# Four message hops that gather neighbours on TensorE instead of by indirect DMA

## The chip, the cores and the metric

The kernel runs on one core of one Trainium2 chip. The metric is the device time of one execution in microseconds (us), lower is better. Before the change three runs gave 6633.33, 6638.75 and 6645.05 us; the median is 6638.75.

## What is computed

A graph has 3125 nodes of 128 features and 100,000 edges `src -> dst`, sorted by `dst`. The reference is an attention layer with five hops of message passing, a feed-forward layer, and three graph convolutions. The part that matters here is this (feature rows `f` are split in 8 heads of 16):

```python
e = leaky_relu(fh[src] * ft[dst], 0.2)           # per edge and head, then a softmax over the edges of a target
a = ex / esum[dst]                               # (100000, 8): one share per edge and head
f = fe
for _ in range(5):
    msg = f[src] * a[:, :, None]                 # gather the source's row, weigh it by head
    agg = segment_sum(msg, dst, num_segments=n)  # sum over the edges of each target
    f = 0.85 * agg + 0.15 * fe
...                                              # layer norm, feed-forward, then three times:
norm = dinv[src] * w * dinv[dst]                 # graph convolution, with self loops
out = segment_sum((x @ W)[src] * norm, dst) + b
```

## The kernel before

**Tiling.** Nodes lie in 25 buckets of 125, one node a partition. Edges, in order of target, are cut into items of 128 edges, one edge a partition, so that every item has targets of one bucket only: 816 items, handled in 204 groups of 4 (51 turns of a loop with 4 slots). For a group, VectorE compares the edges' places in their bucket with a row of numbers, which gives a 128x125 one-hot matrix for each item (`onehots`, L1135). One matmul per item with that matrix as weights (L878) adds the item's 128 message rows into the PSUM columns of its target bucket. The bucket's number is a register that TensorE's instruction stream loads for each group (`buckets_of`, L448). All seven banks hold the sums of a hop; bank 7 is free for other things.

**Stages.** (1) Layer norms, projections, tables. (2) The score stage: per group, GpSimd gathers 4x128 rows of a table by indirect DMA (L673), TensorE turns the one-hots and multiplies, VectorE makes the scores, and the gathered `fe` half is written to a DRAM buffer `edge_fe`. (3) Softmax scans. (4) Hop 0 reads `edge_fe` back group by group through SyncE's queue (L560). (5) Hops 1 to 4: after each hop the new `f` goes to a DRAM table `tab_f`, ScalarE copies the row numbers of a group to `stage` (L736), GpSimd issues four indirect DMAs a group (L673), VectorE makes the one-hots (L1135) and weighs the rows (L1192), TensorE sums. (6) Feed-forward and three convolutions.

**Work tucked into the hops.** The convolutions use a dense adjacency, which is built during hops 1 to 4 in 352 steps, 88 a hop, one with every second group. A step is, on VectorE, one comparison for 4 items (L1150) and four scaled one-hots (L1154), then on TensorE four products (L867), then on VectorE four chained additions (`build_sums`, L1165), each waiting for the one before, and four DMAs to the buffer `adj` (L574). Hop 1 also sums the edge weights of each target with a one-column matmul per item (L875).

**What sets the order.** Each engine's instructions stand in the order of the code, joined by semaphores; there is no planner. [...] 

## Time and profile before

| | |
|---|---|
| Median of three runs | 6638.75 us |
| The profiled execution's own time | 6636.84 us |
| Its span in the trace | 6635.0 us |
| TensorE, VectorE, GpSimd busy | 62%, 53%, 60% of the span |
| Chain that ended last | GpSimd 42%, issue 31%, TensorE 12%, VectorE 7%, DMA 6% |
| Mean granted TensorE clock | 0.607 of full speed |

A busy share is an average over stages with different limits, so the rows below are taken from single stages. In a row, a name such as `L673` is the line of the kernel's file; PE is TensorE, PEld its weight load, DVE is VectorE, ACT is ScalarE, POOL is GpSimd, SP is SyncE, and a q behind an engine's name is its sequencer. [...]

### The profile page before, as it was taken

Reading aid. Unit: us, or ns where it says so; the run is one execution under the profiler, and the core shown is the slowest. Engines: PE = TensorE matmul, PEld = TensorE weight load, DVE = VectorE, ACT = ScalarE, POOL = GpSimd, SP = SyncE. Lnnn points to the kernel's source line nnn. Section 1 sums busy time; section 2 is a strip of 40 time slices with the busy share of each in tenths; the row PEclk is TensorE's granted clock in tenths of the full one; section 3 lists DMA queues with packets and bytes.
Section 4 is the critical chain, followed back from the end, with each engine's and each line's share of the span. In section 5 each row is a group of like instructions: output and inputs, shape, how many; then the busy total and the mean of one; then the engine's idle time right before and its main releaser. Section 6 shows DMA issues by size and latency. Waiting matters only on the chain.

```text
span 6635.0 us, 87679 instructions
## 1 busy us (share of the span) xinstructions
PE 4108.7 (62%) x19868; PEld 3666.2 (55%) x19869; DVE 3545.8 (53%) x7014; ACT 423.6 (6%) x1409; POOL 3995.5 (60%) x4073
## 2 busy tenths in 40 slices
PE   3655645624778888865555544555544555555899
PEld 1444534524668888855545534545443545443899
DVE  7765656677855555435555534555544555544211
ACT  0111111110000000000000000000000000001000
POOL 0577767711047777767777767777776777773000
PEclk9655555557965555555656556565655565656999
DMA  2344464513632222222222212222222222222576
GB/s 58 109 139 146 144 147 135 148 39 117 182 102 77 78 78 77 76 59 77 77 78 77 78 58 76 78 78 77 79 65 68 79 77 78 78 72 76 208 272 231
DMA packets 538438, 671.65 MB, mean 101 GB/s; under 512 B 102388, under 2 KB 423419, under 8 KB 528412
## 3 DMA queue, kind: packets, MB, share of 16 engines
q1 hardware_dynamic: 391970, 345.94, 17.1%
q0 software_dynamic: 143008, 320.73, 16.8%
q10 hardware_dynamic: 3418, 4.48, 0.2%
q8 instruction: 18, 0.29, 0.0%
q14 instruction: 24, 0.20, 0.0%
HBM read 511.17 MB, written 160.80 MB: 101 GB/s over the span
## 4 chain that ended last, share of the span: by engine, by line
POOL 42%; issue 31%; PE 12%; DVE 7%; DMA 6%; SPq 1%; ACT 1%; DVEq 1%; POOLq 0%; ACTq 0%; PEldq 0%; PEld 0%
POOL U L673 42%; PE ps L1091 6%; PE ps L878 3%; DMA U<-edge_fe 2%; DMA U<-tab_f,stage 2%; DVE U L1192 1%; DVE U L1491 1%; DVE U L1463 1%; DVE U L1111 1%; DMA U<-tab_he,stage 1%; PE ps L954 1%; DMA edge_fe<-U 0%; SPq L580 0%; PE ps L867 0%; DMA tab_f<-U 0%
## 5 line engine op out<-in xcount | busy, mean ns | idle before, releaser
L673 POOL DMA_INDIRECT U<-tab_f,stage x3224 | 3102.6, 962 | 1352.6 <-issue 964.1
L878 PE MATMUL ps<-U 128*125 128x128 f32 x8160 | 2051.7, 407 | 1140.3 <-DVE U L1192 1137.4
L878 PEld LDWEIGHTS ps<-U 128*125 128x125 f32 x8160 | 1681.4, 293 | 1282.1 <-issue 1275.9
L1135 DVE TENSOR_TENSOR U<-dloc,iota_p 128x500 f32<-128x500 f32 x1225 | 840.2, 686 | 1974.1 <-DMA U<-tab_f,stage 1919.6
L673 POOL DMA_INDIRECT U<-tab_he,stage x806 | 850.9, 1056 | 438.5 <-issue 246.5
L867 PE MATMUL ps<-gap 128*128 128x125 f32 x2816 | 706.9, 430 | 388.3 <-DVE gap L1165 388.3
L867 PEld LDWEIGHTS ps<-gap 128*128 128x128 f32 x2816 | 630.0, 329 | 460.1 <-issue 460.1
L1192 DVE TENSOR_TENSOR U<-U,ex_it 128x512 f32<-128x512 f32 x1020 | 705.3, 692 | 0.0
L1165 DVE SCALAR_TENSOR_TENSOR gap<-gap,U,ps 128x125 f32<-128x125 f32 x1408 | 483.5, 343 | 154.7 <-DVE gap L1165 79.6
L979 PE MATMUL ps<-U 125*128 x1632 | 422.4, 440 | 210.5 <-ACT U L773 210.5
L875 PEld LDWEIGHTS ps<-w_it,U 128*125 128x125 f32 x1632 | 435.8, 327 | 187.4 <-issue 186.6
L979 PEld LDWEIGHTS ps<-U 125*128 125x128 f32 x1632 | 363.3, 328 | 270.1 <-issue 270.1
L736 ACT COPY stage<-src_it 128x4 int32 (+1 forms) x1023 | 197.6, 193 | 4922.6 <-PE ps L878 4319.9
L875 PE MATMUL ps<-w_it,U 128*125 x1632 | 365.5, 293 | 152.4 <-DVE U L1192 151.9
L972 PE MATMUL ps<-ident,U 128*125 128x128 f32 x816 | 244.1, 454 | 259.1 <-DVE U L1135 258.5
L1154 DVE TENSOR_SCALAR gap<-iota_p,U,raw 128x125 f32<-128x125 f32 x1408 | 389.6, 343 | 0.0
L972 PEld LDWEIGHTS ps<-ident,U 128*125 128x125 f32 x816 | 188.2, 321 | 308.3 <-DVE U L1135 307.3
L1380 DVE TENSOR_TENSOR U<-U,ps 128x512 f32<-128x512 f32 x204 | 140.7, 690 | 378.0 <-DMA U<-tab_he,stage 323.0
L1150 DVE TENSOR_TENSOR gap<-U,iota_p 128x512 f32<-128x512 f32 x352 | 244.2, 694 | 0.2
L1588 DVE TENSOR_TENSOR U<-ps,gap 128x125 f32<-128x125 f32 x75 | 21.7, 289 | 380.9 <-PE ps L1091 380.9
L1091 PE MATMUL ps<-ex_it,U 125*128 125x125 f32 x1500 | 171.5, 274 | 2.3 <-DVE ex_it L1582 2.2
L1091 PE MATMUL ps<-U 125*128 125x125 f32 x1500 | 172.4, 273 | 0.0
(236 smaller groups left out, 2097.1 us busy)
## 6 DMA issues: line engine op xcount, KB each, us to landing
adj<-gap SPq DMA_DIRECT2D x1408, 64.0 KB
edge_fe<-U SPq DMA_DIRECT2D x204, 256.0 KB, 2.5
U<-edge_fe SPq DMA_DIRECT2D x204, 256.0 KB, 2.9
U<-tab_f,stage POOLq DMA_INDIRECT x3224, 2.5
ex_it<-adj SPq DMA_DIRECT2D x30, 1600.0 KB, 6.1
U<-adj SPq DMA_DIRECT2D x30, 1600.0 KB, 6.1
fe_a<-adj SPq DMA_DIRECT2D x15, 1600.0 KB, 6.1
U<-tab_he,stage POOLq DMA_INDIRECT x806, 2.9
```

Source lines behind the costliest of these rows:

```text
L673: pool.indirect_dma_start(to[:, k, j, :], None, table, bass.IndirectOffsetOnAxis(ap=stage[:, k, j:j + 1], axis=0)).then_inc(got[k], 16)
L867: mm = nc.tensor.matmul(ps[:, 7 * BANK + j * CELL:7 * BANK + (j + 1) * CELL], hot_p[:, u, j, :], prod[:, u, j, :], start=True, stop=True)
L875: nc.tensor.matmul(ps[0:BN, bass.ds(b + W_SUMS, 1)], hot[:, k, j, :], w_it[:, bass.ds(r * PER_ITER + (k * G + j), 1)], start=False, stop=F ...
L878: mm = nc.tensor.matmul(ps[0:BN, bass.ds(b * F, F)], hot[:, k, j, :], ga[:, k, j, :], start=False, stop=False, skip_group_check=True)
L972: t = nc.tensor.transpose(bank(k % 2)[0:BN, j * P:(j + 1) * P], hot[:, k, j, :], ident[:])
L979: mm = nc.tensor.matmul(bank(2 + k % 2)[:, j * F:(j + 1) * F], hot_t[:, k % 2, j, :], nb_pad[0:BN, bass.ds(b, 1), :].rearrange("p b f -> p ...
L1091: mm = nc.tensor.matmul(bank(u, BN).rearrange("p (w d) -> p w d", d=WN), rows_[0:BN, b, :], cells[:, :, b, :], start=(b == 0), stop=(b == ...
L1135: return v.tensor_tensor(to[:, (k + ahead) % SLOTS], dloc[:, bass.ds(item_of(r, k, ahead), G)].unsqueeze(2).to_broadcast([P, G, BN]), iota ...
L1150: v.tensor_tensor(hot_p[:, u], win_p[:, bass.ds(i, BG)].unsqueeze(2).to_broadcast([P, BG, P]), iota_p[:].unsqueeze(1).to_broadcast([P, BG, ...
L1154: ins = v.tensor_scalar(prod[:, u, j, :], iota_bn, win_b[:, bass.ds(i, 1)], win_w[:, bass.ds(i, 1)], ALU.is_equal, ALU.mult)
L1165: ins = v.scalar_tensor_tensor(out=win_acc[:, u, j, 0:CELL], in0=before, scalar=win_same[:, bass.ds(win_item(s, r, u, j), 1)], in1=ps[:, 7 ...
L1192: v.tensor_tensor(rows_, rows_, by, ALU.mult).then_inc(msgs_ready, 1)
```

## The change

The edges get a second order, by pair of source bucket and target bucket: 1408 items in place of 816, each with sources of one bucket and targets of one. With it a hop's gather is a product: a one-hot matrix of sources (bf16, 125x128) times the bucket's rows of `f`. `f` is split into three bf16 parts, so an item takes three products, which add up in PSUM bank 7.

- **Score stage**: in its first 25 turns VectorE and TensorE also count each edge's place in the new order (`source_buckets`, `rank_step`, `rank_known`, `places`), and VectorE finds the pairs of the new items (`pair_items`).
- **Hop 0** still reads `edge_fe`. From its 32nd group on, each group is paired with one building step (172 of the 352); the edge weights are summed here. Beside it ScalarE packs the edges' shares, sources and targets into records, and GpSimd scatters these to their new places with 806 indirect DMAs.
- **After hop 0** the 180 steps that are left run by themselves. Then GpSimd gathers the records in the new order (11 DMAs) and TensorE turns them.
- **Hops 1 to 4** no longer use GpSimd. Each is 352 steps of 4 items (`cell_pass`): TensorE gathers the next step's items (12 products) and adds up this step's messages (4 float32 matmuls); VectorE compares sources for every second step, makes the next step's target one-hots, and then weighs the rows that lie in bank 7. Between hops ScalarE and VectorE split `f` (`split_parts`, `split_rest`).

The core of the diff; parts that repeat, buffers and semaphores are left out:

```diff
-            def sum_pass(s):
-                for r0, r1 in ((0, BUILD_ITERS), (BUILD_ITERS, ITERS)) if s else ((0, ITERS),):
-                    sum_groups(s, r0, r1, s > 0 and r0 == 0)
-            def sum_groups(s, r0, r1, building):
+            def build_cells(t, r, k):
+                pe.wait_ge(prod_ready, r * SLOTS + (t + k + 1))
+                pe.wait_ge(acc_ready, r * SLOTS + (t + k + 1))
+                for j in range(BG):
+                    mm = nc.tensor.matmul(cells_at(j), hot_p[:, k % BSLOTS, j, :], prod[:, k % BSLOTS, j, :],
+                                          start=True, stop=True)
+                mm.then_inc(cell_sums, 1)
+            def sum_groups(r0, r1):
                 with pe.Fori(r0, r1) as r:
                     for k in range(SLOTS):
-                        if building and k % 2 == 0:
-                            u = k // 2
-                            pe.wait_ge(prod_ready, r * BSLOTS + (steps_before(s) + u + 1))
-                            pe.wait_ge(acc_ready, r * BSLOTS + (steps_before(s) + u + 1))
-                            for j in range(BG):
-                                mm = nc.tensor.matmul(ps[:, 7 * BANK + j * CELL:7 * BANK + (j + 1) * CELL],
-                                                      hot_p[:, u, j, :], prod[:, u, j, :], start=True, stop=True)
-                            mm.then_inc(cell_sums, 1)
+                        if r0 >= BUILD_FROM:
+                            build_cells(-BUILD_FROM * SLOTS, r, k)
                         buckets = buckets_of(pe, item_of(r, k))
-                        pe.wait_ge(msgs_ready, r * (2 * SLOTS) + (msgs_before(s) + 2 * (k + 1)))
+                        pe.wait_ge(msgs_ready, r * (2 * SLOTS) + (msgs_before(0) + 2 * (k + 1)))
                         for j, b in enumerate(buckets):
-                            if s == 1:
-                                nc.tensor.matmul(ps[0:BN, bass.ds(b + W_SUMS, 1)], hot[:, k, j, :],
-                                                 w_it[:, bass.ds(r * PER_ITER + (k * G + j), 1)],
-                                                 start=False, stop=False, skip_group_check=True)
+                            nc.tensor.matmul(ps[0:BN, bass.ds(b + W_SUMS, 1)], hot[:, k, j, :],
+                                             w_it[:, bass.ds(r * PER_ITER + (k * G + j), 1)],
+                                             start=False, stop=False, skip_group_check=True)
                             mm = nc.tensor.matmul(ps[0:BN, bass.ds(b * F, F)], hot[:, k, j, :], ga[:, k, j, :],
                                                   start=False, stop=False, skip_group_check=True)
                         mm.then_inc(groups_done, 1)
...
+            def cell_pass(s):
+                pe.wait_ge(split_done, BANKS * s)
+                pe.wait_ge(src_hots, (s - 1) * PLOADS + 1 + PRING)
+                gather_items(0, cell_regs(pe, 0))
+                for r0, r1 in cut(0, PITERS - 1, PITERS):
+                    with pe.Fori(r0, r1) as r:
+                        for k in range(PSTEPS):
+                            last = r0 and k == PSTEPS - 1
+                            i = r * (PSTEPS * G) + k * G
+                            of = None if last else cell_regs(pe, i + G)
+                            to = cell_regs(pe, i + PITEMS)
+                            pe.wait_ge(weighted, group_of(s, r, k) + 1)
+                            if not last:
+                                if k % 2:
+                                    pe.wait_ge(src_hots, load_of(s, r, (k + 1) // 2) + (1 + PRING))
+                                gather_items((k + 1) % PSTEPS, of)
+                            pe.wait_ge(dst_hots, group_of(s, r, k) + 1)
+                            for j, b in enumerate(to):
+                                mm = nc.tensor.matmul(ps[0:BN, bass.ds(b * F, F)], dst_hot[:, k % PRING, j, :],
+                                                      msg[:, k % PRING, j, :], start=False, stop=False,
+                                                      skip_group_check=True)
+                            mm.then_inc(scattered, 1)
+            def gather_items(k, cells):
+                for j, b in enumerate(cells):
+                    for n in range(PARTS_F):
+                        mm = nc.tensor.matmul(bank(7)[:, j * F:(j + 1) * F], src_t[0:BN, k // 2, k % 2 * G + j, :],
+                                              split[0:BN, n, bass.ds(b, 1), :].rearrange("p b f -> p (b f)"),
+                                              start=(n == 0), stop=(n == PARTS_F - 1))
+                mm.then_inc(gathered, 1)
...
+            def rank_step(r):
+                pe.wait_ge(rank_hot, r + (1 - RANK_FROM))
+                for n, m in enumerate((before_m, ones_b)):
+                    for half in range(2):
+                        mm = nc.tensor.matmul(bank(4 + 2 * n + half, HALF), m[:], src_hot[:, half * HALF:(half + 1) * HALF],
+                                              start=True, stop=True)
+                mm.then_inc(rank_sums, 1)
...
-            def message_pass(s):
-                for r0, r1 in cut(0, 1, FULL_ITERS, BUILD_ITERS, ITERS) if s else cut(0, ITERS):
-                    if s and r0 == BUILD_ITERS:
-                        build_sums(s, BUILD_ITERS - 1, BSLOTS - 1)
-                    message_groups(s, r0, r1, s > 0 and r0 < BUILD_ITERS)
-                dve.wait_ge(groups_done, SLOTS + (s + 1) * GROUPS)
...
-            def message_groups(s, r0, r1, building):
+                dve.wait_ge(acc_ready, r * SLOTS + (t + k + 2))
+            def message_groups(r0, r1):
+                t = -BUILD_FROM * SLOTS
                 with dve.Fori(r0, r1) as r:
                     for k in range(SLOTS):
-                        if building and k % 2 == 0:
-                            build_factors(s, r, k // 2)
-                            if k or r0:
-                                build_sums(s, r if k else r - 1, (k // 2 - 1) % BSLOTS)
-                        if s == 0:
-                            dve.wait_ge(loaded[k], r * 16 + 16)
-                        else:
-                            dve.wait_ge(got[k], got_at(s, r, k, r0))
+                        if r0 >= BUILD_FROM:
+                            build_factors(t, r, k)
+                            if k or r0 > BUILD_FROM:
+                                build_sums(t, r, k - 1)
+                        dve.wait_ge(loaded[k], r * 16 + 16)
                         onehots(hot, r, k).then_inc(msgs_ready, 1)
                         i = item_of(r, k)
                         rows_ = ga[:, k].rearrange("p g (h d) -> p (g h) d", h=HEADS)
                         by = ex_it[:, bass.ds(i, G), :].rearrange("p g h -> p (g h)").unsqueeze(2).to_broadcast(
                             [P, G * HEADS, HD])
                         v.tensor_tensor(rows_, rows_, by, ALU.mult).then_inc(msgs_ready, 1)
+            def compare_sources(s, r, q, ahead=0):
+                dve.wait_ge(loaded[(q + ahead) % PRING], r * 16 + 16 * (ITERS + (s - 1) * PITERS + 1 + (q + ahead) // PRING))
+                dve.wait_ge(gathered, 2 * load_of(s, r, q + ahead) + 2)
+                v.tensor_scalar(src_t[0:BN, (q + ahead) % PRING].rearrange("p i e -> p (i e)"),
+                                ids[0:BN, (q + ahead) % PRING, :], pidx[0:BN, 0:1], None,
+                                ALU.is_equal).then_inc(src_hots, 1)
+            def dst_onehots(s, r, k, ahead=0):
+                dve.wait_ge(scattered, group_of(s, r, k + ahead) + 1)
+                v.tensor_tensor(dst_hot[:, (k + ahead) % PRING],
+                                dst_c[:, bass.ds(r * (PSTEPS * G) + (k + ahead) * G, G)].unsqueeze(2).to_broadcast([P, G, BN]),
+                                iota_bn.unsqueeze(1).to_broadcast([P, G, BN]), ALU.is_equal).then_inc(dst_hots, 1)
+            def weigh(s, r, k):
+                dve.wait_ge(gathered, group_of(s, r, k) + (1 + 2 * PRING))
+                dve.wait_ge(scattered, group_of(s, r, k) + 1)
+                by = ex_it[:, bass.ds(r * (PSTEPS * G) + k * G, G), :].rearrange("p g h -> p (g h)").unsqueeze(
+                    2).to_broadcast([P, G * HEADS, HD])
+                v.tensor_tensor(msg[:, k % PRING].rearrange("p g (h d) -> p (g h) d", h=HEADS),
+                                bank(7).rearrange("p (x d) -> p x d", d=HD), by, ALU.mult).then_inc(weighted, 1)
+            def cell_pass(s):
+                compare_sources(s, 0, 0)
+                dst_onehots(s, 0, 0)
+                for r0, r1 in cut(0, PITERS - 1, PITERS):
+                    with dve.Fori(r0, r1) as r:
+                        for k in range(PSTEPS):
+                            if k % 2 == 0 and not (r0 and k == PSTEPS - 2):
+                                compare_sources(s, r, k // 2, 1)
+                            if not (r0 and k == PSTEPS - 1):
+                                dst_onehots(s, r, k, 1)
+                            weigh(s, r, k)
+                dve.wait_ge(scattered, PRING + s * PGROUPS)
+            def split_rest(n):
+                def part_of(k):
+                    b0, b1 = bank_buckets(k)
+                    return b0, b1, rest[0:BN, k, 0:(b1 - b0) * F].rearrange("p (b f) -> p b f", f=F)
+                for k in range(BANKS):
+                    b0, b1, to = part_of(k)
+                    dve.wait_ge(split_high, n * BANKS + k + 1)
+                    v.tensor_tensor(to, na[0:BN, b0:b1], split[0:BN, 0, b0:b1], ALU.subtract).then_inc(split_link, 1)
+                for k in range(BANKS):
+                    b0, b1, to = part_of(k)
+                    dve.wait_ge(split_mid, n * BANKS + k + 1)
+                    v.tensor_tensor(split[0:BN, 2, b0:b1], to, split[0:BN, 1, b0:b1], ALU.subtract).then_inc(split_done, 1)
+                dve.wait_ge(split_done, (n + 1) * BANKS)
...```

[...]

```order
L448 ISA
L448 TENSOR_LOAD bucket_row
L872 REGISTER_ALU
L878 ISA
L878 MATMUL ps<-U 125x128
```

TensorE, one step of hops 1 to 4 now, from the last of the four adding matmuls (L1103) of one step to the first of the twelve gathering products (L1112) of the next:

```order
L1103 ISA
L1103 MATMUL ps<-U 125x128
L553 ISA
L553 TENSOR_LOAD U
L553 ISA
L553 TENSOR_LOAD U
L1096 REGISTER_ALU
L1099 ISA
L1112 ISA
L1112 MATMUL ps<-U 128x128
```

A step now has two register loads, for the source and the target buckets, and 16 matmuls, each behind a register instruction of its own; a group before had one load and four.

VectorE, hop 0, the end of a building step and a message group, then the next step's beginning (L1425 are the chained additions, L1402 the one-hots, L1449 the weighting, L1409 and L1413 the factors of the next step). In the kernel before, hop 0 has the lines L1135 and L1192 alone, which are L1402 and L1449 here.

```order
L1425 ISA
L1425 SCALAR_TENSOR_TENSOR gap<-gap,U,ps 128x125
L1432 REGISTER_ALU
L1402 ISA
L1402 TENSOR_TENSOR U<-dloc,iota_p 128x500
L1449 ISA
L1449 TENSOR_TENSOR U<-U,ex_it 128x512
L1409 ISA
L1409 TENSOR_TENSOR gap<-U,iota_p 128x512
L1413 ISA
L1413 TENSOR_SCALAR gap<-iota_p,U,raw 128x125
```

The building step has moved from every second group of hops 1 to 4 to every group of hop 0 from the 32nd on.

## Rows read from the trace of the kernel before

**Rows 1.** The profile page, groups of instructions: busy, mean ns | idle before, releaser

```profile
L673 POOL DMA_INDIRECT U<-tab_f,stage x3224 | 3102.6, 962 | 1352.6 <-issue 964.1
```

**Rows 2.** Waits, all engines: us in total, times, longest

```profile
DVE U L1135 <- DMA U<-tab_f,stage: 1919.6, 811, 19.8
```

**Rows 3.** Chain that ended last, in order of time: ends of hops 0 and 4

```profile
1878.83 3.88 DVE U L1534 x7
...
6060.52 3.89 DVE U L1534 x7
```

**Rows 4.** Windows: hop 0, part of hop 1, hop 2, convolutions

```profile
core 0: us, PE busy (x) PEld busy (x) DVE busy (x) ACT busy (x) POOL busy (x), PEclk, DMA share, GB/s
1550.00:1885.00 335.00, 241.36 (x1635) 203.50 (x1635) 280.96 (x420) 0.77 (x4) 22.46 (x11) 0.93 0.58 171
2205.00:2525.00 320.00, 281.27 (x1271) 272.04 (x1271) 174.52 (x414) 12.18 (x63) 242.91 (x254) 0.50 0.28 78
2930.00:3980.00 1050.00, 565.62 (x2357) 503.33 (x2355) 524.29 (x1212) 39.95 (x207) 776.66 (x806) 0.56 0.26 74
6168.00:6635.00 467.00, 449.50 (x3948) 443.88 (x3947) 64.24 (x232) 30.09 (x76) 0.00 (x0) 0.99 0.67 249
```

**Rows 5.** Sequencer instructions by line, 1605.2 to 1606.4 us (hop 0, one group)

```profile
L878 PEldq FUSED_REGOPS  x4: 46/46/46, 1605.3 to 1605.7; - x4
...
L448 PEldq FUSED_REGOPS  x1: 46/46/46, 1605.8 to 1605.8; - x1
L448 PEldq TENSOR_LOAD <-bucket_row x1: 334/334/334, 1605.9 to 1605.9; - x1
...
L872 PEldq ALU_OP  x1: 32/32/32, 1606.3 to 1606.3; - x1
```

**Rows 6.** The same for L979, 600 to 604 us (score stage, one group)

```profile
L979 PEldq FUSED_REGOPS  x4: 55/55/55, 602.7 to 603.1; - x4
```

**Rows 7.** Timeline of hop 0: start us, us, engine line op

```profile
1601.13 0.67 DVE L1135 TENSOR_TENSOR U<-dloc,iota_p 128x500 f32<-128x500 f32 x1
...
1601.72 0.68 DVE L1192 TENSOR_TENSOR U<-U,ex_it 128x512 f32<-128x512 f32 x1
1602.33 0.67 DVE L1135 TENSOR_TENSOR U<-dloc,iota_p 128x500 f32<-128x500 f32 x1
```

**Rows 8.** Timeline of hop 2, a group with a building step

```profile
3200.59 0.68 DVE L1150 TENSOR_TENSOR gap<-U,iota_p 128x512 f32<-128x512 f32 x1
...
3202.22 0.34 DVE L1165 SCALAR_TENSOR_TENSOR gap<-gap,U,ps 128x125 f32<-128x125 f32 x1
3202.71 1.33 DVE L1165 SCALAR_TENSOR_TENSOR gap<-gap,U,ps 128x125 f32<-128x125 f32 x3 [0.15 <-DVE gap L1165]
...
3204.18 2.04 PE L867 MATMUL ps<-gap 128*128 128x125 f32 x8 [1.29 <-DVE gap L1165]
```

**Rows 9.** Timeline of hop 1, TensorE: two items with the weight column

```profile
2302.60 0.77 PE L878 MATMUL ps<-U 128*125 128x128 f32 x2
...
2303.45 0.77 PE L878 MATMUL ps<-U 128*125 128x128 f32 x2
```

**Rows 10.** Timeline, TensorE: clearing seven banks after hop 0

```profile
1882.76 3.16 PE L851 MATMUL ps<-zeros 1*128 1x512 bf16 x7 [8.94 <-DVE U L1534]
```

**Rows 11.** Timeline of the score stage: VectorE's last and first work of a group

```profile
599.43 0.69 DVE L1389 TENSOR_REDUCE ex_it<-U 128x512 f32 x1
...
604.95 0.69 DVE L1389 TENSOR_REDUCE ex_it<-U 128x512 f32 x1
```

**Rows 12.** Groups of instructions with shapes kept apart: the nearest to the new ones

```profile
L1463 DVE TENSOR_TENSOR_SCAN U<-gap,U 128x6528 f32<-128x6528 bf16 x3 | 41.3, 13758 | 9.5 <-ACT U L793 9.4
...
L1277 DVE TENSOR_SCALAR_CACHE_REDUCE U<-U 128x782 f32<-128x782 f32 x25 | 24.2, 968 | 0.9
...
L1417 DVE TENSOR_SCALAR_CACHE_REDUCE U<-U,win_it 128x625 f32<-128x625 f32 x11 | 9.5, 864 | 0.4
...
L1029 PE MATMUL ps<-ident,U 128*128 128x128 f32 x51 | 8.1, 336 | 23.3 <-ACT U L806 23.3
```

More of the change, by code:

```diff
@@ L44 @@
 AHEAD = SLOTS - 1
-TABLES = HOPS - 1
 WN = 5
@@ new lines, in _ @@
+            with sp.Fori(0, BUILD_FROM + 1) as r:
+                for k in range(SLOTS):
+                    load_group(r, k)
+            sp.wait_ge(targets_ready, 1)
+            first = -(BUILD_FROM + 1) * SLOTS
+            with sp.Fori(BUILD_FROM + 1, ITERS) as r:
+                for k in range(SLOTS):
+                    load_group(r, k)
+                    store_step(first, r, k)
+            sp.wait_ge(cell_out, 16 * 2)
+            sp.dma_start(cell_row, cell_d.rearrange("(a n) -> a n", a=1)).then_inc(cell_in, 16)
@@ new lines, in _ @@
+            act.wait_ge(built, 1)
+            for k in range(PK):
+                act.wait_ge(rec_turned, k + 1)
+                at_ = slice(k * P, (k + 1) * P)
+                banks = [3 * (k % 2) + n for n in range(3)]
+                nc.scalar.copy(ex_it[:, at_, HALF_HEADS:], bank(banks[1]).rearrange("p (h i) -> p i h", i=P)
+                               ).then_inc(rec_kept_a, 1)
+                nc.scalar.copy(dst_c[:, at_], bank(banks[2], P)).then_inc(rec_kept_a, 1)
+            for s in range(HOPS - 1):
+                split_parts(s)
```

509 lines of the change are left out of this document (416 added, 93 removed).

## The prediction

> **What bounds the kernel now.** I read the chain of waits first, then the page's groups, then windows by stage, then the timeline of one group in each stage. From the end of hop 0 to the end of hop 4 the trace takes 6060.5 - 1878.8 = 4182 us [rows 3], two thirds of the span. There GpSimd sets the pace: an indirect DMA costs it (3102.6 + 964.1) / 3224 = 1.26 us with its issue gap [rows 1], so 806 of them are 1017 us, nearly a whole hop. VectorE mostly waits for those rows, 1920 us in all [rows 2], and in hop 2 it is busy 524 of 1050 us, with the building steps in it [rows 4]. So the building is free today, and hop 0, which does without GpSimd, takes about 335 us [rows 4]. The change takes GpSimd out of hops 1 to 4. What counts is what a step of the new hops costs on TensorE and VectorE, and what the building costs once nothing covers it.
>
> **The new step of hops 1 to 4.** There are 352 steps a hop.
>
> VectorE has one 500-element comparison and one 512-element weighting. These start 0.6 us apart when nothing holds them [rows 7]. The source comparison, 1024 bf16 elements in every second step, is not in the trace: at the pace of the 6528-element scan it would be the dearest, 2.1 ns an element or 2.2 us, at the 782-element comparison's it is 1.24 ns or 1.3 us [rows 12], so at most 0.65 to 1.1 us a step. VectorE needs 1.5 to 2.3 us a step.
>
> TensorE's array has 12 bf16 products of 128 columns and 4 float32 matmuls, which are 8 halves. [...]
>
> TensorE's sequencer has the most. In one group of hop 0 its rows can be followed: four register instructions that stand ahead of a matmul each, from 1605.3 to 1605.7, then at 1605.8 the register instruction of the load, the load itself at 1605.9 (334 ns) and the next instruction at 1606.3 [rows 5]. So a matmul with a register costs 0.125 us of sequencer time, and a load 0.5 us, whatever the array does. In the score stage, where the register picks the operand that streams through, as in the new gather, four such rows stand from 602.7 to 603.1 and last 55 ns instead of 46 [rows 6], which makes 0.133 us. The new step has two loads, 12 gathering products with a register each, and 4 adding matmuls with one each; the wait values and the loop's end add some 0.15 us (I take 0.1 us for each register instruction that stands alone). The sum is 2 x 0.5 + 12 x 0.133 + 4 x 0.125 + 0.15 = 3.25 us. A group of the kernel before needs 4 x 0.125 + 0.5 + 0.1 = 1.1 us, which lies below VectorE's 1.2 us, so nothing waits for it today.
>
> The round trip must fit too, since there is one bank for gathered rows: weighting 0.69 us, the release of TensorE (3204.04 to 3204.18, 0.14 [rows 8]), the 12 products as the sequencer issues them, 1.6 us, and some 0.4 us until the last is done and VectorE starts: 2.8 us, below 3.25. I take 3.25 us a step, the sequencer's sum. From below 3.0 us (0.115 us a product and no standing instructions), from above 3.6 us (waits that I don't see).
>
> [...]
>
> A hop is 352 x 3.25 = 1144 us, and between hops come the sums, the two halves of the split, and the first gather. That is 21 instructions of VectorE at 0.6 us, since ScalarE's copies run beside them, and about 5 us until the first weighting: 18 us. Four hops: 4 x 1162 = 4648 us against 4182, **+466 us**. The gather by products is no faster than the gather by DMA.
>
> **The building loses its cover.** On VectorE a step runs from 3200.59 to 3204.04 [rows 8], and 0.2 us more until the next instruction can start: 3.7 us. With the message group's 1.2 us that is 4.9 us a group of hop 0. TensorE in the same group has four items with the weight column, 0.85 us each at 1.2 GHz [rows 9], and the four products, 8 halves or 1.7 us, together 5.1. In hop 1, the only stretch with these three kinds of work, the granted clock is 0.50 throughout [rows 4], so I take 5.2 us for 172 groups, and 3.4 us for the 32 without a step: 894 + 109 + 5 = 1008 us against 335 [rows 4], less 2 us of lead: **+675 us**. At 2.4 GHz VectorE would set 4.9 us, and the 32 groups take 56 us, together 113 us less.
>
> The 180 steps after hop 0 pass the work to and fro: the additions need the products, the products the additions before. Additions 1.82 us (3202.22 to 3204.04), 0.14 until TensorE starts, products 2.04 us [rows 8], 0.1 back: 4.1 us, while the factors of the next step are made beside the products. 180 x 4.1 = **+738 us**; at 2.4 GHz 3.7 us and 72 us less. Nothing else runs then that the end depends on: the 806 scatters need 806 x 1.26 = 1016 us from hop 0's start on GpSimd and end before this building does, so I cost them at nothing. They would show only if a scatter took over twice as long.
>
> **Smaller terms.** Counting in the score stage: per turn, for 25 turns, two scans of 408 elements at 2.1 ns [rows 12] and six passes over 408 to 816 elements at about 1.1 to 1.2 ns, some 7 us. A turn is four groups of 5.5 us, of which VectorE spends five instructions of about 0.7 us each [rows 11], 3.5 us a group: room for 8 us, so these are hidden in the main. Not hidden are 13 passes over 816 elements ahead of the first group, 12 us, and the search for the pairs, 11 comparisons at 0.9 us [rows 12] and some 25 small instructions, 25 us, of which GpSimd's lead of three groups hides a part; with places in between I take **+60 us**, from 20 to 130. Records: 11 rounds, each nine turns on TensorE at 0.3 us [rows 12], copies and a DMA: **+50 us**, from 25 to 80. The tail loads `x` later, and two small instructions stand alone: **+7 us**.
>
> **Sum.** 466 + 675 + 738 + 60 + 50 + 7 = 1996 us. The profiled execution took 6636.84 us, 0.03% off the median shown, so 8633 us: **8630 us**, slower by 30%. With all low ends (3.0 us a step, 2.4 GHz in the building, the small terms low) 8030 us; with the high ends 9220 us. As they will not all fall together, the likeliest case's own range is 8200 to 9050 us.
>
> **Rivals.**
>
> *The array sets the step, not the sequencer.* If register instructions were worked off ahead while matmuls wait, the step would be the round trip with products at array pace: 0.69 + 0.14 + 12 x 0.054 + 0.4 = 1.9 us to, at a float32 half's 0.12 us each, 2.7. Half-way, 2.3 us, gives 8633 - 0.95 x 1408 = 7300 us. For it speaks that the sequencer runs ahead of the array in hop 0; against it that its rows stand 0.125 us apart even then [rows 5]. Chance 0.07. [...]
>
> *The step is a chain.* If the sequencer can't prepare the next loads while VectorE weighs, because the wait for the target one-hots or the four matmuls holds it, the round trip and the rest add up: 2.8 + 0.5 + 1.0 = 4.3 us, 8633 + 1.05 x 1408 = 10,110 us. Against it: the order has the loads ahead of the wait for the weighting. Chance 0.05.
>
> *Faster.* The register work is hidden as in the first rival, and TensorE keeps 2.4 GHz from hop 0 to hop 4, so that the step is 1.85 us and the building loses 185 us: 8633 - 1.4 x 1408 - 185 - 40 = 6440 us. The point from which the change pays is a step of 1.83 us with the other terms as they stand, 2.0 us with these low. For it speaks that hop 0 ran at 0.93 [rows 4]; against it the spacing of the sequencer's rows again. Chance 0.04.
>
> **How the numbers follow.** The sequencer's case has 0.84; the rivals 0.07, 0.05 and 0.04. The range 8100 to 9100 leaves out all three rivals, 0.16, and the far ends of the likeliest case, about 0.04. A change within 0.2% is what a measurement of this kernel can't tell from none. Faster by over 0.2%: 0.04. Within 0.2%: 0.01, a step of 1.83 us by chance. Slower: 0.95.
>
> **What would show it.** In the changed profile: a pass of 352 steps takes 1050 to 1200 us with VectorE and the array busy about half of it; the matmuls of the gather start some 0.13 us apart, and between two steps TensorE's array sits idle behind its own sequencer and not behind VectorE; hop 0 takes about 1000 us, the building after it some 740 us with TensorE and VectorE in turns, and GpSimd's scatters end before it. The forecast is wrong if a step takes under 2.8 us, if waits for VectorE's weighting lead the list of TensorE's waits, or if the scatters are what hop 0 or the records wait for.

## The result, and the profile after

The changed kernel takes 8699.5 us (median of 4 runs, 8694.9 to 8705.2), the kernel before 6636.9 us on the same chip: a ratio of 1.311, 95% interval 1.308 to 1.313. The forecast was 8630 us.

The span is cut by events that both traces have: the first weighting of hop 0, the bank sums that end a hop, the first split, the end. The two first weightings are these rows, of the kernel before and of the changed one (the columns: line, engine, operation, tiles, count: ns shortest/median/longest, first and last start in us).

```profile
L1192 DVE TENSOR_TENSOR U<-U,ex_it x1020: 679/686/3631, 1548.1 to 6057.6; 128x512 f32<-128x512 f32 x170
```

```profile
L1449 DVE TENSOR_TENSOR U<-U,ex_it x204: 680/686/3648, 1623.8 to 2608.2; 128x512 f32<-128x512 f32 x102
```

Hop 0 starts 76 us later. The changed kernel's chain of waits (start, us, what) gives the ends of hop 0 and of hop 4, beside [rows 3], and what follows hop 4:

```profile
2614.15 3.88 DVE U L1977 x7
```

```profile
8091.54 3.89 DVE U L1977 x7
8095.51 34.15 DMA U<-in_x
```

Its stages by windows: hop 0, the building after it, a part of hop 3, the load of `x`, the convolutions. Beside [rows 4] the reader sees a hop 0 three times as long at a clock of 0.50 in place of 0.93, and hops at the full clock (1.00) in which VectorE is busy 45% of the time. TensorE's 578 of 700 us there is no measure of what its array needs: each gathering product stands in the trace for 228 ns, and with fixed buckets (below) the same products start 0.056 us apart.

```profile
core 0: us, PE busy (x) PEld busy (x) DVE busy (x) ACT busy (x) POOL busy (x), PEclk, DMA share, GB/s
1623.00:2614.00 991.00, 986.32 (x4647) 984.01 (x4645) 794.62 (x1956) 91.06 (x724) 769.90 (x721) 0.50 0.40 105
2618.00:3385.00 767.00, 368.91 (x1448) 322.15 (x1448) 559.33 (x1628) 12.95 (x90) 95.80 (x96) 0.50 0.22 64
5000.00:5700.00 700.00, 577.75 (x4266) 449.80 (x4266) 314.82 (x534) 0.00 (x0) 0.00 (x0) 1.00 0.10 39
8097.00:8130.00 33.00, 0.00 (x0) 0.00 (x0) 2.06 (x1) 0.00 (x0) 0.00 (x0) 0.50 0.67 242
8230.00:8696.00 466.00, 449.48 (x3948) 443.85 (x3947) 63.99 (x232) 30.07 (x76) 0.00 (x0) 0.99 0.67 250
```

The list of waits now, beside [rows 2] (us in total, times, longest):

```profile
DVE U L1472 <- PE ps L1112: 2539.1, 1408, 2.6
...
PEld ps L1112 <- issue: 1086.3, 1412, 7.1
...
PE ps L1112 <- DVE U L1455: 418.3, 696, 6.2
...
PE ps L1112 <- issue: 397.9, 701, 1.2
```

VectorE waits 1.8 us a step for the gathering products. What TensorE waits for is put down to its own issue in one half of the steps and to VectorE's source comparison in the other. The timeline of one step lets that be judged; each float32 matmul stands in it as two halves, each with a weight load (L1103, 8 and 8 for four), each bf16 one as one with one (L1112, 12 and 12):

```profile
5000.51 0.69 DVE L1472 TENSOR_TENSOR U<-ps,ex_it 128x512 f32<-128x512 f32 x1 [2.22 <-PE ps L1112]
5001.12 0.48 DVE L1455 TENSOR_SCALAR U<-gap,pidx 125x1024 bf16<-125x1024 bf16 x1
...
5001.98 1.53 PEld L1112 LDWEIGHTS ps<-U 125*128 125x128 bf16 x12 [0.77 <-issue]
5001.99 1.67 PE L1112 MATMUL ps<-U 125*128 x12 [0.59 <-DVE U L1455]
5003.54 0.95 PEld L1103 LDWEIGHTS ps<-U 128*125 128x125 f32 x8
5003.55 1.14 PE L1103 MATMUL ps<-U 128*125 128x128 f32 x8
5003.80 0.69 DVE L1472 TENSOR_TENSOR U<-ps,ex_it 128x512 f32<-128x512 f32 x1 [1.61 <-PE ps L1112]
```

and the rows of TensorE's sequencer in the same stretch, first the loads, then the instruction that sets the value of the wait for the comparison, then the gathering products, as [rows 5] showed them for hop 0:

```profile
L553 PEldq FUSED_REGOPS  x2: 46/46/46, 5000.7 to 5001.2; - x2
L553 PEldq TENSOR_LOAD <-U x2: 332/332/333, 5000.8 to 5001.3; - x2
```

```profile
L1099 PEldq FUSED_REGOPS  x1: 42/42/42, 5001.8 to 5001.8; - x1
```

```profile
L1112 PEldq FUSED_REGOPS  x12: 46/46/60, 5001.9 to 5003.3; - x12
```

The weighting was done at 5001.20 and the comparison at 5001.60, both before the sequencer came to the waits for them (L1099, 5001.8); the gather began at 5001.98, when the second load (5001.3, 332 ns) and the standing instructions behind it were through. Then the twelve register instructions follow, 0.13 us apart (0.131 us from product to product in the mean of all 1408 gathers), and the next four and two loads behind them. In the whole step of 3.28 us the sequencer has no stretch in which it waits. "<-DVE U L1455" names only the last semaphore that came. The sequencer's rows stand in the order in which the code has the lines: L553, L1096 (5001.7), L1099, L1112, L1103 (5003.4 to 5003.9). What the listing of the change has there as `REGISTER_ALU` is an ALU_OP of 32 to 36 ns in them (L1096), and `ISA` a FUSED_REGOPS.

### The profile page after: what moved, and what is told of

It reads as the page before. It is cut to its first block, busy times and chain, and to the rows that moved or that the text cites. A ratio compares the mean times of both kernels' runs of the same rounds, so it can differ in the third digit from the quotient of the medians.

```text
span 8696.7 us, 162184 instructions
## 1 busy us (share of the span) xinstructions
PE 6497.5 (75%) x41703; PEld 5403.9 (62%) x41704; DVE 4863.9 (56%) x9329; ACT 406.2 (5%) x1487; POOL 1742.2 (20%) x1671
## 4 chain that ended last, share of the span: by engine, by line
PE 60%; DVE 15%; issue 15%; POOL 3%; DVEq 3%; DMA 2%; ACT 1%; SPq 1%; POOLq 0%; ACTq 0%; PEldq 0%; PEld 0%
PE ps L1112 27%; PE ps L1103 9%; PE ps L1049 7%; PE ps L1065 6%; PE ps L1358 5%; DVE U L1455 4%; POOL U L821 3%; DVE gap L1425 3%; PE ps L1062 2%; PE ps L1227 2%; PE ps L1220 1%; DVE U L1472 1%; DVE U L1933 1%; DVE U L1905 1%; DMA U<-tab_he,stage 1%
## 5 line engine op out<-in xcount | busy, mean ns | idle before, releaser
L1112 PE MATMUL ps<-U 125*128 x16896 | 2355.1, 228 | 821.4 <-DVE U L1455 418.3
L1112 PEld LDWEIGHTS ps<-U 125*128 125x128 bf16 x16896 | 1628.3, 96 | 1627.0 <-issue 1086.3
L1472 DVE TENSOR_TENSOR U<-ps,ex_it 128x512 f32<-128x512 f32 x1408 | 975.9, 693 | 2539.1 <-PE ps L1112 2539.1
L1103 PE MATMUL ps<-U 128*125 128x128 f32 x11264 | 1607.2, 284 | 0.0
L1103 PEld LDWEIGHTS ps<-U 128*125 128x125 f32 x11264 | 1345.7, 187 | 44.9 <-issue 0.2
L1462 DVE TENSOR_TENSOR U<-raw,iota_p 128x500 f32<-128x500 f32 x1408 | 946.2, 672 | 0.0
L869 POOL DMA_INDIRECT rec_d<-ex_it,stage x806 | 844.8, 1048 | 245.6 <-issue 230.6
L1425 DVE SCALAR_TENSOR_TENSOR gap<-gap,U,ps 128x125 f32<-128x125 f32 x1408 | 487.2, 346 | 272.8 <-PE ps L1049 100.5
L1065 PE MATMUL ps<-U 128*125 128x128 f32 x1632 | 628.1, 489 | 0.0
L1227 PE MATMUL ps<-U 125*128 x1632 | 407.8, 429 | 213.6 <-ACT U L930 213.6
L1065 PEld LDWEIGHTS ps<-U 128*125 128x125 f32 x1632 | 443.1, 332 | 0.0
L1413 DVE TENSOR_SCALAR gap<-iota_p,U,raw 128x125 f32<-128x125 f32 x1408 | 388.5, 346 | 0.0
L1062 PE MATMUL ps<-w_it,U 128*125 x1632 | 344.3, 280 | 4.6 <-DVE U L1449 4.6
L1455 DVE TENSOR_SCALAR U<-gap,pidx 125x1024 bf16<-125x1024 bf16 x704 | 337.2, 479 | 0.1
L1402 DVE TENSOR_TENSOR U<-dloc,iota_p 128x500 f32<-128x500 f32 x409 | 282.5, 691 | 87.1 <-DMA U<-edge_fe 54.4
```

Source lines behind the costliest of these rows:

```text
L869: pool.indirect_dma_start(rec_d, bass.IndirectOffsetOnAxis(ap=stage[:, k, j:j + 1], axis=0), recs[:, k, j, :], None).then_inc(got[k], 16)
L1062: nc.tensor.matmul(ps[0:BN, bass.ds(b + W_SUMS, 1)], hot[:, k, j, :], w_it[:, bass.ds(r * PER_ITER + (k * G + j), 1)], start=False, stop=F ...
L1065: mm = nc.tensor.matmul(ps[0:BN, bass.ds(b * F, F)], hot[:, k, j, :], ga[:, k, j, :], start=False, stop=False, skip_group_check=True)
L1103: mm = nc.tensor.matmul(ps[0:BN, bass.ds(b * F, F)], dst_hot[:, k % PRING, j, :], msg[:, k % PRING, j, :], start=False, stop=False, skip_g ...
L1112: mm = nc.tensor.matmul(bank(7)[:, j * F:(j + 1) * F], src_t[0:BN, k // 2, k % 2 * G + j, :], split[0:BN, n, bass.ds(b, 1), :].rearrange(" ...
L1227: mm = nc.tensor.matmul(bank(2 + k % 2)[:, j * F:(j + 1) * F], hot_t[:, k % 2, j, :], nb_pad[0:BN, bass.ds(b, 1), :].rearrange("p b f -> p ...
```

## The experiments

All later runs were on chips where the kernel before took 6682 to 6710 us, and most were single runs. So the length of a step is read within each trace: from the first to the last of a hop's 352 weightings, divided by 351. In the changed kernel it is 3.278 us, and 3.28 in the three runs below that leave these hops as they are (no building, two banks, `x` early).

The theory (A) is the forecast's: TensorE's sequencer sets the step. The rivals: the array sets it (B), or the wait for VectorE's comparison does (C).

**Fixed buckets, both.**

```
-  gather_items(0, cell_regs(pe, 0))
+  gather_items(0, range(G))
   ...
-  of = None if last else cell_regs(pe, i + G)
-  to = cell_regs(pe, i + PITEMS)
+  of = range(G)
+  to = range(G)
```

> Hops 1 to 4 take fixed buckets (0 to 3) in all their products; no bucket number is read into a register. It leaves out that the right buckets are gathered from and added to; counts and sizes of products, waits, VectorE's work and DMAs stay. Theory A (TensorE's sequencer sets the step of 3.26 us: two register loads and 16 register instructions): these go, and what is left is the round trip through the one gather bank, 0.69 (weighting) + 0.14 (release) + 12 products at 0.06 to 0.08 + 0.4 = 2.0 to 2.3 us a step, total 7000 to 7350 us. Rival B (TensorE's array sets it, or the clock): no change, 8700 us. Rival C (the odd steps wait for VectorE's source comparison, as the list of waits says of L1455): no change, 8650 to 8700 us.

6617.9 us; the step is 1.791 us. The twelve gathering products of one step, with the same array work:

```profile
L1112 PEld LDWEIGHTS ps<-U x12: 97/98/100, 4502.2 to 4502.7; 125*128 125x128 bf16 x12
```

They stand 0.056 us apart instead of 0.131, at the same granted clock of 1.00, and the line has no row of the sequencer left (FUSED_REGOPS x12 in the changed kernel). The step and the total lie under the ranges I gave (2.0 to 2.3 us a step). What is left is the round trip: 0.69 us of weighting, 0.05 (even steps) or 0.13 (odd steps) until the first product, 0.85 for the twelve, 0.15 until VectorE starts. VectorE is now busy 2115 of 2566 us in the hops. B and C fall: the array's work, the comparison and its wait were all left in.

**Fixed buckets, gather alone.** `of` and the first gather take `range(G)`, `to` stays.

> Only the gathering products of hops 1 to 4 take fixed buckets; the adding products keep their registers and one load a step. It leaves out that the right source buckets are gathered. Theory A: one load of 0.5 us and 12 register instructions of 0.129 us go; the sequencer needs 0.5 + 4 x 0.125 + 12 x 0.06 to 0.08 + 0.2 = 1.9 to 2.2 us, the round trip is as with both fixed, so a step of 2.1 to 2.3 us, 7050 to 7350 us, nearly as with both fixed. Rivals B and C: no change, 8650 to 8700 us.

6614.3 us, a step of 1.790 us, as with both fixed and as far under the range. One load and four register instructions a step cost nothing once the gather's are gone: the sequencer is then under the round trip.

**Fixed buckets, adding products alone.** Only `to` takes `range(G)`.

> Only the adding products of hops 1 to 4 take fixed buckets; the gathering keeps its 12 register instructions and one load a step. It leaves out that the sums go to the right target buckets. Theory A by the sequencer's sum alone: 0.5 of the load and some 0.3 of the four register instructions go, step 2.45 us, 7570 us. Theory A with the round trip as the next limit (weighting 0.69 + release 0.14 + two standing instructions 0.2 + 12 products at 0.129 + 0.4 = 2.9 us): the gain stops at 0.35 us a step, 8150 to 8250 us. Rivals B and C: 8650 to 8700 us.

7920.1 us, a step of 2.723 us. The gain is 0.55 us a step: more than the 0.35 that I gave for the round trip, less than the 0.8 of the sequencer's sum. The round trip is there, but 2.7 us, not 2.9: in the median 2.68 us in even steps and 2.76 in odd ones, which have one wait more. Here is an even one; the gather begins 0.15 us after the weighting's end.

```profile
4501.28 0.69 DVE L1472 TENSOR_TENSOR U<-ps,ex_it 128x512 f32<-128x512 f32 x1 [1.06 <-PE ps L1112]
...
4502.12 1.51 PEld L1112 LDWEIGHTS ps<-U 125*128 125x128 bf16 x12 [0.25 <-issue]
...
4503.92 0.69 DVE L1472 TENSOR_TENSOR U<-ps,ex_it 128x512 f32<-128x512 f32 x1 [1.36 <-PE ps L1112]
```

**One part.**

```
-  for n in range(PARTS_F):
+  for n in range(1):
   ...
-      start=(n == 0), stop=(n == PARTS_F - 1))
+      start=(n == 0), stop=True)
```

> The gather makes one bf16 product an item in place of three; it leaves out the two lower parts of the numbers gathered. Theory A: 8 register instructions of 0.129 us less a step, 3.26 - 1.03 = 2.2 us, 7200 to 7300 us, and now the sequencer alone is the limit (the round trip is 1.85 us). Rival B (array): 8 x 0.054 = 0.43 us a step, 8090 us. Rival C: at most the time to the comparison, no change in the odd steps, 8300 us or more.

7267.0 us, a step of 2.26 us. Eight products fewer take 1.02 us off, 0.128 us each: the price of the register instruction, more than twice the array's 0.056.

**Loads of eight.**

```
-  of = None if last else cell_regs(pe, i + G)
-  to = cell_regs(pe, i + PITEMS)
+  if k % 2 == 0:
+      of2 = cell_regs(pe, i + G, 2 * G)
+  of = of2[k % 2 * G:][:G]
+  if k % 2 or k == 0:
+      to2 = cell_regs(pe, i + PITEMS, G if k in (0, PSTEPS - 1) else 2 * G)
+  to = to2[G:] if k and k % 2 == 0 else to2[:G]
```

> The bucket numbers of two steps come by one load of eight registers: one load a step in place of two, alternately for the gathering and the adding products. The computation is whole. Theory A (TensorE's sequencer): a load costs 0.5 us whatever it fetches, so its sum falls from 3.28 to 2.78 us a step; the round trip through the gather bank, 2.72 us as the run with only the adding products fixed showed it, lies just below. Total 8699 - 0.5 x 1408 = 8000 us (7950 to 8080). If a load's cost grows with the registers (0.125 us each) nothing is gained, 8700 us. Rival (the wait for VectorE's source comparison): 8650 to 8700 us.

8425.4 us, a step of 3.075 us: 0.20 us gained instead of 0.50. The row of one load shows why:

```profile
L553 PEldq TENSOR_LOAD <-U x1: 588/588/588, 5001.7 to 5001.7; - x1
```

588 ns for eight registers against 332 for four: 0.064 us a register on top of some 0.08, and 0.19 us between its neighbours and it as before. I had the cost of a load as one number; half of it grows with its length. By these rows 0.24 us a step should be gained; the last 0.04 stay open.

**No building.** The factors, products and additions are taken out of hop 0 and of the loop after it.

> Leaves out the factors, products and additions of all 352 building steps; the stores of the steps are still sent, with old contents. By the terms of the forecast alone: 180 steps after hop 0 go (767 us) and hop 0 falls from 991 to some 340 us, total 8699 - 767 - 650 = 7280 us. But GpSimd's 806 scatters, about 1090 us from hop 0's start, then stand bare, since the records need them: if they do, the first split starts some 1150 us after hop 0's start in place of 1800, total 8050 us (7950 to 8150).

8170.1 us; both sums fail. Hop 0 takes 735 us (1637.6 to 2372.8), not 340, and the first split stands at 2894.0, 1256 us after hop 0's start. Two of its windows, inside hop 0 and behind it (columns as above):

```profile
2000.00:2100.00 100.00, 97.17 (x442) 94.03 (x442) 36.05 (x56) 9.06 (x72) 77.75 (x74) 0.50 0.59 149
...
2373.00:2850.00 477.00, 1.95 (x8) 1.58 (x8) 4.21 (x9) 37.44 (x282) 276.44 (x286) 0.50 0.37 104
```

In hop 0 TensorE is 97% busy at a granted clock of 0.50 with the messages and the weight column alone, 3.6 us a group, though no building is there. And after it the stores set the end, not the scatters, which end at 2733.7:

```profile
DVE dinv L1986 <- DMA adj<-gap: 476.4, 1, 476.4
```

The 180 steps' stores take 2.65 us a step by themselves, no less after the scatters' end (2.69) than beside them (2.64). So of the 660 us by which hop 0 grew, the building makes 255 (990 - 735); 405 are left in hop 0 without it, where TensorE is the limit: the weight column, which the change moves there, and the lower clock together. No run separates the two. From hop 0's start to the first split it is 1256 us here against 1801 in the changed kernel, so faster building could gain at most 545 us as long as its stores are sent as they are.

**Two banks in the building.** Products of even steps go to bank 6, so that they need not wait for the additions of the step before (the additions read the same bank):

```
-  pe.wait_ge(acc_ready, r * SLOTS + (t + k + 1))
+  pe.wait_ge(acc_ready, r * SLOTS + (t + k + 1 - two))
   ...
-      mm = nc.tensor.matmul(cells_at(j), ...
+      mm = nc.tensor.matmul(cells_at(j, 6 if two and k % 2 == 0 else 7), ...
```

> In the 180 building steps after hop 0 the products of even steps go to bank 6 (free then) and those of odd steps to bank 7, so that TensorE's products of a step stand beside VectorE's additions of the step before. The computation is whole. If work passed to and fro is what makes 4.26 us a step, VectorE alone sets it: 3.7 us, 180 x 0.56 = 100 us less, 8600 us (8570 to 8640), the stretch from hop 0 to the records 665 us in place of 767. If VectorE's own chain was the limit already, or the stores are, no change, 8700 us.

8612.6 us; from the hop's sums to the last addition 674 us (2624.0 to 3298.3), 3.75 us a step. That is the time of VectorE's own chain, as forecast, and the difference to 4.28 is what the passing to and fro cost.

**`x` early.**

```
+  act.dma_start(x_sb[1:BN], nodes_of(a["x"])[1:BN]).then_inc(x_again, 16)
   act.wait_ge(hops_done, 1)
-  act.dma_start(x_sb[0:BN], nodes_of(a["x"])).then_inc(x_again, 16)
+  act.dma_start(x_sb[0:1], nodes_of(a["x"])[0:1]).then_inc(x_again, 16)
   ...
-  dve.wait_ge(x_again, 16)
+  dve.wait_ge(x_again, 32)
```

> Rows 1 to 124 of x are loaded while hop 4 runs (the bucket numbers lie only in row 0); row 0 after the hops. The computation is whole. The tail's load of 34 us, which stands bare behind the last sum, falls to some 3 us: 30 us less, 8668 us; from the last sum to the end 575 us in place of 605. If the load's time lay in its own fixed cost, 5 us or less.

8677.2 us; from the last sum to the end 580.7 us, 24.4 less. The one row still costs 7.5 us:

```profile
8098.63 7.49 DMA U<-in_x
```

**The registers on ScalarE.** The fixed gather pointed to a form that keeps the computation: ScalarE, idle in the hops, reads the source bucket's register and copies the bucket's three parts into a ring of four steps, and TensorE gathers from fixed places in it. The next four runs have this, the two banks and the early `x`.

```
   ...
+  of = cell_regs(eng, i + js[0], len(js))
+  eng.wait_ge(gathered, group_of(s, r, k) + (1 + 2 * PRING - PRING))
+  for j, b in zip(js, of):
+      copy(held[0:BN, k % PRING, j], split[0:BN, 0:HELD, bass.ds(b, 1), :]...).then_inc(done, 1)
   ...
-  split[0:BN, n, bass.ds(b, 1), :].rearrange("p b f -> p (b f)"),
+  held[0:BN, k % PRING, j, n, :],
```

With GpSimd copying the fourth item:

> The source bucket's registers move off TensorE: ScalarE (three items of a step) and GpSimd (one) copy the three bf16 parts of an item's source bucket into a ring of four steps, and TensorE gathers from fixed places in it; it reads registers for the adding products alone. With it the two banks in the building and the early load of x. The computation is whole. Theory A (TensorE's sequencer was the limit of the hops, and VectorE with the round trip is the next, 1.79 us a step as the runs with fixed buckets showed): ScalarE's three copies of 384 elements at 0.48 us are 1.45 us and fit, so the step is 1.8 us and the total 8699 - 1.48 x 1408 - 88 - 24 = 6500 us (6450 to 6600), 2% under the kernel before. Rival: the copies become the pace (GpSimd's copy over 1.8 us, or VectorE slowed by it): a step of 2.0 to 2.4 us, 6780 to 7350 us.

6748.9 us against 6693.6, ratio 1.008 (1.006 to 1.010): no gain, and above the 6450 to 6600 us that I gave. The step is 1.97 us instead of 1.8. With ScalarE copying all four:

> The three-part form with ScalarE copying all four items of a step. The computation is whole. ScalarE's copies of 384 elements, 0.48 us each, are 1.93 us a step and become the pace: a step of 1.95 to 2.1 us, 8699 - 1.23 x 1408 - 112 = 6850 us (6730 to 6900). If ScalarE's register load of 0.5 us isn't hidden beside its copies, 2.45 us a step, 7420 us.

6614.9 us (one run), a step of 1.88 us: better than with the help, and under the 1.95 us at which ScalarE's copies were to set the pace. Two rows of ScalarE's and GpSimd's copies in the run with both:

```profile
L1033 ACT COPY U<-U 125x384 bf16 x4224 | 1882.3, 509 | 893.5 <-PE ps L1153 877.3
...
L897 POOL COPY U<-U 125x384 bf16 x1408 | 719.4, 511 | 2115.4 <-PE ps L1153 2038.9
```

Neither engine is the pace there: both wait for TensorE. What differs is one more wait in TensorE's queue, between the weighting's end and the gather. An even step with both buckets fixed, where nothing stands between the two, and an odd step of the run with both copying engines, where three waits do (source one-hots and two semaphores of the copies):

```profile
4501.41 0.69 DVE L1472 TENSOR_TENSOR U<-ps,ex_it 128x512 f32<-128x512 f32 x1
...
4502.16 0.67 PEld L1112 LDWEIGHTS ps<-U 125*128 125x128 bf16 x12 [0.15 <-DVE U L1472]
```

```profile
4502.49 0.69 DVE L1514 TENSOR_TENSOR U<-ps,ex_it 128x512 f32<-128x512 f32 x1 [0.63 <-PE ps L1153]
...
4503.50 0.67 PEld L1153 LDWEIGHTS ps<-U 125*128 125x128 bf16 x12 [0.41 <-POOL U L897]
```

From the weighting's end to the first product it is 0.05 us with none between, 0.32 with three; with one it is 0.13 (fixed buckets, odd steps) and with two 0.22 (ScalarE alone, odd steps). Each costs 0.07 to 0.10 us, and "<-POOL" again names only the last semaphore. Take this stretch off the median step, and 1.69 us is left in even and odd steps of all four runs (both buckets fixed, the gather's fixed, both engines copying, ScalarE alone). So the round trip sets the step in all of them, and not the copies; nor does GpSimd's help slow VectorE, whose weighting takes 693 ns with it and without. The last run tests it.

With one part and ScalarE:

> The same with ScalarE alone and one bf16 part an item in place of three; it leaves out the two lower parts of the numbers gathered, and the splitting of them. ScalarE needs 4 x 0.29 = 1.2 us a step, TensorE's sequencer 0.52 + 4 x 0.125 + 4 x 0.06 + 0.3 = 1.6 us, VectorE 0.6 + 0.6 + 0.2 = 1.4 to 1.6 us. Theory A: a step of 1.65 us, total 8699 - 1.63 x 1408 - 88 - 24 - 40 = 6250 us (6200 to 6450). Rival: VectorE and the round trip do not get below the 1.79 us of the fixed buckets: 6450 us or more.

6049.9 us against 6693.6, ratio 0.904 (0.903 to 0.906), a step of 1.49 us. That is under the range I gave. VectorE is busy 1930 of 2025 us of the hops, and its three kinds of work stand nearly without a gap:

```profile
4201.29 0.48 DVE L1477 TENSOR_SCALAR U<-gap,pidx 125x1024 bf16<-125x1024 bf16 x1
4201.68 0.67 DVE L1484 TENSOR_TENSOR U<-raw,iota_p 128x500 f32<-128x500 f32 x1
4202.27 0.68 DVE L1494 TENSOR_TENSOR U<-ps,ex_it 128x512 f32<-128x512 f32 x1
4202.87 0.67 DVE L1484 TENSOR_TENSOR U<-raw,iota_p 128x500 f32<-128x500 f32 x1
4203.63 0.69 DVE L1494 TENSOR_TENSOR U<-ps,ex_it 128x512 f32<-128x512 f32 x1
```

In the steps with a source comparison VectorE now sets the pace (1.59 us); in the others it still waits some 0.1 us for the gather (4203.54 to 4203.63). I had its step at 1.4 to 1.6 us and still took 1.65.

With the wait for the weighting put last:

```
-  pe.wait_ge(weighted, group_of(s, r, k) + 1)
   if not last:
       ...
       held_wait(group_of(s, r, k) + 1)
+  pe.wait_ge(weighted, group_of(s, r, k) + 1)
```

> The three-part form with ScalarE copying all items, and TensorE's waits for the copies and for the source one-hots put ahead of the wait for the weighting, so that only the last stands in the round trip. The computation is whole. The weighting's end to the first gathering product was 0.23 us there (4501.35 to 4501.58) and 0.13 to 0.16 us with both buckets fixed. Theory A: each standing wait costs the sequencer 0.1 us, and in the round trip this is paid in full; the step falls from 1.88 to 1.79 us, 127 us, total 6490 us (6460 to 6550), ratio to before 0.970. Rival: ScalarE, 93% busy with its copies in the hops, is the pace already: a step of 1.85 us or more, 6570 to 6620 us.

6544.5 us against 6685.4 (5 and 9 runs), ratio 0.978 (0.977 to 0.980): the whole computation, and faster than both kernels. The step is 1.83 us: 0.05 us gained, half of what the theory gave. The other half is not the rival's. The groups of ScalarE's copies without and with the edit:

```profile
L1018 ACT COPY U<-U 125x384 bf16 x5632 | 2459.5, 508 | 188.4 <-PE ps L1138 142.3
```

```profile
L1018 ACT COPY U<-U 125x384 bf16 x5632 | 2459.9, 508 | 117.2 <-PE ps L1139 29.0
```

ScalarE is busy 95% of its time now, and yet it isn't the limit. All of its 117 us of idle time lie ahead of the first of a step's four copies, a little in nearly every step. That copy starts together with VectorE's weighting, when TensorE's gather is done and has left a place in the ring; the four then take 1.75 us:

```profile
4502.06 0.51 ACT L1018 COPY U<-U 125x384 bf16 x1
4502.07 0.69 DVE L1500 TENSOR_TENSOR U<-ps,ex_it 128x512 f32<-128x512 f32 x1 [0.54 <-PE ps L1139]
```

```profile
4502.06 1.75 ACT L1018 COPY U<-U 125x384 bf16 x4
```

They start 0.41 us apart, not the 0.48 that I had taken. In the first nine or more steps of each hop, until the ring is full, ScalarE goes at its own pace, 1.65 us a step and without a gap; from then on it waits, and keeps TensorE's 1.81. What is left stands in TensorE's queue. The wait for the weighting (L1120) is still an instruction of its own ahead of the first product:

```profile
4500.26 0.69 DVE L1500 TENSOR_TENSOR U<-ps,ex_it 128x512 f32<-128x512 f32 x1
...
4501.07 0.69 PEld L1139 LDWEIGHTS ps<-U 125*128 125x128 bf16 x12 [0.21 <-issue]
```

```profile
L1120 PEldq EVENT_SEMAPHORE  x1: 51/51/51, 4501.0 to 4501.0; - x1
```

From the weighting's end to the first product it is 0.115 us in even and odd steps alike, where it was 0.13 and 0.22; the rest of the step is 1.70 us, much as in the other runs. The round trip is still the limit.

## Why the prediction was right

The forecast was 69 us under the result, 0.8%. By its own terms, whose measured values add up to the difference of the spans (8696.7 against 6635.0, 2062 us); the six miss by +19, -15, +33, +16, -10 and +24 us, so no large errors cancel:

- **The step of the hops: 3.25 us forecast, 3.28 measured.** Hops 1 to 4 take 3424.6 to 8091.5 = 4667 us against 4182, +485 (forecast +466). The parts of the sum are in the trace as they were read from hop 0: loads of 0.52 us each, gathering products 0.131 us apart, adding products 0.125. That this sum was the limit, and not merely equal to it, the runs show: take away registers and the step falls to 1.79 us with all array work left in; take away eight of sixteen register products and it falls by eight times their price (1.02 us, 0.128 each). A product without a register takes 0.056 us, with its weight load, in the run with fixed buckets.
- **The round trip: 2.8 us forecast, 2.7 measured** in the run with the adding products fixed. It lies under the sequencer's sum, as forecast, and it is what keeps a saving in the queue from paying in full. VectorE's share was over-sized, without weight for the sum: the source comparison takes 0.48 us and not 1.3 to 2.2, so VectorE needs some 1.4 us a step and not 1.5 to 2.3.
- **Hop 0: +675 forecast, +660 measured** (990 against 331). The number held and so did its two parts: the forecast has 3.4 us a group for messages and weight column at the lower clock and some 1.8 for the building; the run without building shows 3.6 us and 990 - 735 = 255 us for the 172 steps, 1.5 each. What I named it, "the building loses its cover", was wrong for the larger part: most of the 660 us is the weight column and the lower clock (0.50 in place of 0.93), which the forecast had in its sum but not under that name.
- **Building after hop 0: +738 forecast, +771 measured**, 4.28 us a step instead of 4.1. The to and fro is shown by the two banks.
- **Scatters at nothing: right**, they end at 2740, the building at 3385. But what waits behind the building is not the scatters: the stores would stand there next.
- **Score stage +60, measured +76; records +50, measured +40.** Within their bounds.
- **The tail: +7 forecast, +31 measured.** This term was mis-sized. I counted the instructions around the late load of `x` and not the load: 34.15 us stand bare on the chain. Only the first row of `x`, whose place holds the bucket numbers, has to wait for the hops; loading the rest of it early took 24 us back.

Some terms of the forecast's sums no run shows. No row gives a clock in GHz: for the 1.2 of the sums the traces have a granted clock of 0.50, in hop 0 and in the building after it, and for the 2.4 one of 0.99 to 1.00, in hops 1 to 4. No run has the building at the full clock, so the 113 and 72 us less that the sums give for it are not shown. The 0.054 us a product of the array's rival and of what I expected with one part has no row behind it, nor have the 0.06 to 0.08 of what I expected with fixed buckets; there the products start 0.056 us apart. A float32 half takes 0.21 us at 0.50 [rows 9] and 0.12 at 0.99 [rows 4].

The rivals: the array at its own pace (7300 us) and the faster case (6440 us) would have needed the sequencer to work ahead; the run with fixed buckets is what that would have been, and it lands at 6618 us, with a step of 1.79 us where the rivals had 2.3 and 1.85. The longer chain (4.3 us a step) fell with the step itself.

Not settled: why the granted clock in hop 0 stays at 0.50. The rows say that before the change TensorE was busy 72% of hop 0 at 0.93 [rows 4], after it 99.5% at 0.50, and without building 97% at 0.50; no run set these apart.

## What to carry to other kernels

Here a matmul whose address comes from a register was paid in the sequencer (0.131 us), not in the array (0.056 us or less): count the register instructions and loads of a step, price them from the spacing of the sequencer's rows, and compare that with the round trip and the busiest engine before anything else. If the sequencer is the bound, let an idle engine do the indexing and give TensorE fixed addresses; then put the wait that comes last, last in the queue (0.05 us a step here). A busy share near 100% doesn't make an engine the limit (ScalarE at 95% was not): look whether it waits at the start of every step, and for whom. And when a step is moved to a later place, ask of each of its DMAs what it will lie beside there.

## What the runs showed of the hardware

- Twelve bf16 products of 128 columns stand 0.056 us apart with fixed addresses and 0.131 with a register each (the run with both buckets fixed, the changed kernel), both at a granted clock of 0.99 to 1.00.
- A register load takes 332 ns for four registers (the changed kernel) and 588 for eight (the run with loads of eight).
- A wait instruction between the last wait and the first product cost TensorE 0.07 to 0.10 us in four runs (0.05, 0.13, 0.22 and 0.32 us with none, one, two and three), even where what it waits for is long there.
- GpSimd copies 384 bf16 elements of 125 partitions in 511 ns, ScalarE in 509 (the run with both copying); ScalarE's start 0.41 us apart in a row (the last run).
- Stores of 64 KB, four a step, take 2.65 us a step when nothing else paces them (the run without building).
